# First halves of x and W0 turned by TensorE, every 4th channel in a k tile, and product 5 by output tile, in a two-layer LoRA kernel on one core

## The chip, the cores and the metric

The kernel runs on one core of one Trainium2 chip. The metric is the device time of one execution in microseconds (us); lower is better. The time of a kernel is the median over its runs.

## The reference

Two layers are applied one after the other to x, 8 rows of 256 tokens with 1024 channels, all in float32:

```
x = x + L0(x): base = x @ W.T                    # W: 1024 x 1024
      logits = x @ Wr.T + 5 * one_hot(language)  # 8 experts
      gates  = softmax over the two largest logits, 0 for the other experts
      lora   = ((x @ A[e].T) * gates[e]) @ B[e].T summed over e   # rank 16
      L0     = base + 2 * lora
x = x + x @ weight[adapter_id].T                 # one of 16 matrices, 1024 x 1024, for each of the 8 rows
```

## The kernel before, in words

**Precision.** Every operand of a large product is split into a high part (ScalarE copies it to the rounded matmul type, `high`, L965) and a low part (VectorE subtracts the high part, `low`, L583). A product step is three matmuls of 128x128 by 128x512: high by high, high by low, low by high (L1227 to L1229). Where a term is its own input added on (`x +`), ones are added to the diagonal of the weight matrix (`add_diagonal`, L572; for the second layer `add_ones` on GpSimd, L501).

**Layer 0.** The 2048 tokens are worked in two spans of 1024. Within a span the 1024 x 1024 by 1024 x 1024 product is cut into halves in each direction and done by a Strassen scheme with seven products, in the order 1, 2, 6, 7, 5, 4, 3. Each product has four output tiles r and four k tiles k, so 16 steps of 3 matmuls. Of span 0, products 1, 2 and 6 run r outside and k inside ("by tile", the rest run k outside and need all four weight pieces of the product at their first step). s1 to s4 and t1 to t4 are the sums and differences of the quarters of W0 and x that the scheme wants. `features` (L1220) computes x @ A.T and the logits with full float32 matmuls; `make_gates` makes the gates on VectorE; `turn_gated` (L1259) turns the gated features on TensorE, `gT_high` and `gT_low` split them (L987, L692), and `lora` (L1238 to L1241) adds the low-rank part to a quarter. `add_up` (L715) adds a finished quarter's parts, `copy_u3` (L1007) copies a bank out.

**Channels on the partitions.** Both operands need the channel of the contraction on the partitions. Rows of x, W0, A, Wr and of the second layer's matrices are loaded in four bands of 256 channels, each to its 32 partitions (`fill`, `fill_x`, L421 and L428), and VectorE turns 32x32 blocks (STREAM_TRANSPOSE, L545 for halves, L566 for whole tiles, L559 and L759 for A and Wr, L730 for the second layer). k tile m holds the channels q*256 + m*32 + j, and a block's 32 channels lie side by side.

**Start.** TensorE runs 30 matmuls on the identity (`WARM`, L1206). The first halves of the four x tiles and of W0's tile 0 are loaded by the queues of SyncE and ScalarE, turned by VectorE (`turn_half`, L545), split, and product 1 starts. While product 1 runs, W0's tiles 1 to 3 come one by one: VectorE turns a tile, adds the diagonal, and it is split.

**Layer 1.** 64 tiles of the chosen matrices are loaded by SyncE's queue, get their diagonal on GpSimd, are turned (L730) and split (L1066 on ScalarE, L736 on VectorE). VectorE gives one tile the pair L730 and L736. The result of layer 0 comes back from HBM and is split too (L1057, L720). For each row and each half of the outputs there are two output tiles of 24 matmuls (L1349 to L1351), which need the four tiles of their group. ScalarE copies results out (L1083) and stores them.

All engines run lists written out by hand, in order; the order of VectorE's and ScalarE's lists is the schedule.

Of the kernel before, what the change touches and what calls it, by code (L numbers as in the profile page):

```python
# [5 lines left out]
def cond_resid_kernel(nc, x, lang_ids, adapter_ids, w0, wr, a, b, w1, out):  # L6
# [7 lines left out]
    NB, T, D = x.shape  # L14
    E, R, _ = a.shape
    NA = w1.shape[0]
    P = 128
# [14 lines left out]
    WARM = 30  # L32
# [15 lines left out]
    def by_tile(s, i):  # L48
        return s == 0 and i in (1, 2, 6)
# [9 lines left out]
    def x_item(s, h, t):  # L59
# [14 lines left out]
    FRONT = ([("xh", t, 0) for t in range(XT)] + [("wh", 0, 0)] + [("w", r) for r in range(1, HM)] + [("a",)] +  # L74
             [("xh", t, 1) for t in range(XT)] + [("wh", 0, 1)])
# [6 lines left out]
    SLOT["wh", 0, 0] = SLOT["wh", 0, 1] = W0_PLACES[0]  # L82
# [17 lines left out]
    for i in (5, 4, 3):  # L100
        PIECES += [("bd",)] if i == 4 else []
        PIECES += [("u", i, r) for r in range(HM)] + [("x", 0, i, k) for k in range(HM)]
# [24 lines left out]
    with ctx:  # L127
# [104 lines left out]
        def sides(p):  # L232

            kind = p[0]
            if kind in ("xl", "xr"):
                t, h = p[1], kind == "xr"
                cut, ms = slice(t * P, (t + 1) * P), slice(h * HM, (h + 1) * HM)
                return (half_x(0, t, h).rearrange("p (m f) -> p m f", m=HM), early_hi[:, ms, cut], early_lo[:, ms, cut])
            if kind in ("wl", "wr"):
                i, r = (1, p[1]) if kind == "wl" else (2, p[1])  # L240
                return turned_wf[:, r, (i - 1) * HALF:i * HALF], u_whole(i, 0)[:, r], u_whole(i, 1)[:, r]
# [33 lines left out]

        def b_ps():
            return banks[:, 4:6, :]
# [17 lines left out]
        x_loaded = [[sem(f"x{'lr'[h]}{pair}_loaded") for h in range(2)] for pair in range(2)]  # L295
        w_half_loaded = [sem(f"w0{'lr'[h]}_loaded") for h in range(2)]
# [119 lines left out]
        def x_raw(t):  # L416
            return turned_wf[:, HM + t]

        def fill(engine, slot, rows, signal, parts=range(Q), j=slice(0, DQ)):
            for c in parts:  # L420
                engine.dma_start(raw_tile(slot)[c * S:(c + 1) * S, :].rearrange("p (q j) -> p q j", q=Q)[:, :, j],  # L421
                                 rows[:, :, c * DQ:(c + 1) * DQ][:, :, j]).then_inc(signal, 16)

        def fill_x(engine, pair, h, parts=range(Q)):
            rows = x_rows[pair * 2 * P:(pair + 1) * 2 * P, :].rearrange("(n s) d -> s n d", s=S)
            for c in parts:
                dst = turned_wf[c * S:(c + 1) * S, HM + 2 * pair:HM + 2 * pair + 2, :]
                engine.dma_start(dst.rearrange("p t (q j) -> p (t q) j", q=Q)[:, :, h * P:(h + 1) * P],  # L428
                                 rows[:, :, c * DQ + h * P:c * DQ + (h + 1) * P]).then_inc(x_loaded[pair][h], 16)

        def fill_w_half(engine, h, parts=range(Q)):
            fill(engine, W0_PLACES[0], w0_rows(0), w_half_loaded[h], parts, slice(h * P, (h + 1) * P))

        def w0_rows(m):
            return w0.rearrange("(q m s) d -> m s q d", m=M, s=S)[m]
# [4 lines left out]
        def _(sp):  # L440
# [27 lines left out]
            fill_x(sp, 0, 0, (0, 1))  # L468
            fill_x(sp, 1, 0, (0, 1))
            fill_w_half(sp, 0, (0, 1))  # L470
# [3 lines left out]
            fill_x(sp, 0, 1)  # L474
            fill_x(sp, 1, 1)
            fill_w_half(sp, 1)
# [8 lines left out]
        def _(pool):  # L485
# [28 lines left out]
            def make_s3(r):  # L514
                pool.wait_ge(transposed, TURN_AT["w", HM + r] + 1)
                pool.wait_ge(lo_done, PIECE_AT["wl", r] + 1)
                if r == 0:
                    pool.wait_ge(t2_done, XT)
# [16 lines left out]
        def _(dve):  # L535
            def turn_half(item):
                kind, n, h = item
                if kind == "xh":
                    dve.wait_ge(x_loaded[n // 2][h], Q * 16)
                    src, dst = x_raw(n), tokens_f[:, n]  # L540
                else:
                    dve.wait_ge(w_half_loaded[h], Q * 16)
                    src, dst = raw_tile(SLOT[item]), turned_wf[:, n]
                ms = slice(h * HM, (h + 1) * HM)
                nc.vector.transpose(dst.rearrange("p (m q s) -> p q m s", m=M, q=Q)[:, :, ms],  # L545
                                    src.rearrange("p (q m j) -> p q m j", q=Q, m=M)[:, :, ms]).then_inc(transposed, 1)

            def turn(item):
# [9 lines left out]
                if item[0] == "a":  # L558
                    nc.vector.transpose(fac[:, :, 0:ER].rearrange("p m (q s) -> p q m s", q=Q),  # L559
                                        src.rearrange("p (q m j) -> p q m j", q=Q, m=M)).then_inc(transposed, 1)  # L560
# [5 lines left out]
                nc.vector.transpose(dst.rearrange("p (m q s) -> p q m s", m=M, q=Q),  # L566
                                    src.rearrange("p (q m j) -> p q m j", q=Q, m=M)).then_inc(transposed, 1)

            def add_diagonal(m):
                dve.wait_ge(transposed, TURN_AT[("w", m) if m else ("wh", 0, 0)] + 1)  # L570
                ones = turned_wf[:, m, m * P:(m + 1) * P]
# [151 lines left out]
            def turn_w1(n):  # L723
# [15 lines left out]
            turn_half(("xh", 0, 0))  # L739
            turn_half(("xh", 1, 0))  # L740
            low(("xl", 0))
            low(("xl", 1))
            turn_half(("xh", 2, 0))
            turn_half(("xh", 3, 0))
            low(("xl", 2))
            turn_half(("wh", 0, 0))
# [632 lines left out]
```

## Time and profile before

| | |
|---|---|
| median of 3 runs | 404.14 us (402.94 to 404.2) |
| the profiled execution | 401.46 us, its span 399.7 us |
| TensorE busy | 391.1 us, 98% |
| VectorE busy | 310.2 us, 78% |
| ScalarE busy | 173.8 us, 43% |
| GpSimd busy | 52.9 us, 13% |
| granted TensorE clock | 1.0 |

The span is what the trace covers, from 0 to 399.7 us; the execution's own time is 1.8 us longer. A busy share is the time in which an instruction of the engine was in work. Matmuls overlap, so each is listed with a longer duration than the step from one to the next.

### The profile page before, as it was taken

The numbers are of one execution on the slowest core, as the hardware profiler recorded it, in microseconds if no ns is written. First come the engines' busy times: TensorE is split into PE (matmuls) and PEld (weight loads), VectorE is DVE, ScalarE is ACT, GpSimd is POOL, SyncE is SP. The second block draws the span as 40 slices with busy tenths as digits, with TensorE's granted clock in tenths as the row PEclk, the third lists the DMA queues.
The fourth block names the chain that finished last, engine by engine and source line by source line (L and its number), as shares of the span: only waits on it lengthen the run. The fifth ranks groups of instructions, "written<-read, shape, count | busy, mean of one in ns | idle before, by whom it ended". The sixth has DMA issues, their size and how long they took to land.

```text
span 399.7 us, 5958 instructions
## 1 busy us (share of the span) xinstructions
PE 391.1 (98%) x1900; PEld 330.0 (83%) x1900; DVE 310.2 (78%) x419; ACT 173.8 (43%) x245; POOL 52.9 (13%) x81
## 2 busy tenths in 40 slices
PE   8899999799999999999999999999999999999996
PEld 8698988588889888888888888878888888888886
DVE  5899998997457568229877956999999999999900
ACT  3352263754220143335355333655555555656511
POOL 1005300000000100000110211442232120323000
PEclk9999999999999999999999999999999999999999
DMA  9998750033476400006492999999999999999232
GB/s 208 227 200 209 106 161 2 0 107 106 137 202 204 91 1 0 2 0 197 136 289 117 229 261 247 281 250 267 271 274 282 266 277 282 272 260 235 66 93 52
DMA packets 87553, 68.60 MB, mean 172 GB/s; under 512 B 16322, under 2 KB 86498, under 8 KB 87010
## 3 DMA queue, kind: packets, MB, share of 16 engines
q1 hardware_dynamic: 60832, 46.55, 49.8%
q10 hardware_dynamic: 26690, 21.67, 18.3%
q8 instruction: 15, 0.25, 0.3%
q14 instruction: 16, 0.13, 0.1%
HBM read 53.51 MB, written 14.68 MB: 171 GB/s over the span
## 4 chain that ended last, share of the span: by engine, by line
PE 94%; DVE 2%; ACT 1%; DMA 1%; issue 0%; ACTq 0%; DVEq 0%
PE banks L1349 15%; PE banks L1350 15%; PE banks L1351 15%; PE banks L1227 13%; PE banks L1228 12%; PE banks L1229 12%; PE banks L1220 7%; PE banks L1238 2%; PE banks L1240 2%; PE banks L1241 2%; DMA turned_w_f<-in_x_dram 1%; DVE weights L583 1%; ACT weights L965 0%; DVE turned_w_f L628 0%; PE banks L1259 0%; DVE tokens_f L545 0%
## 5 line engine op out<-in xcount | busy, mean ns | idle before, releaser
L1227 PE MATMUL banks<-ring,weights 128*128 128x512 f32 x192 | 75.2, 392 | 2.4 <-DVE stage L715 2.4
L1349 PE MATMUL banks<-weights,tokens 128*128 128x512 f32 (+1 forms) x184 | 70.0, 380 | 0.0
L1351 PE MATMUL banks<-weights,tokens 128*128 128x512 f32 (+1 forms) x184 | 69.9, 380 | 0.0
L1350 PE MATMUL banks<-weights,tokens 128*128 128x512 f32 (+1 forms) x184 | 69.9, 380 | 0.0
L1066 ACT ACTIVATE weights<-weights_f 128x1024 fp32r<-128x1024 f32 x44 | 46.5, 1060 | 52.7 <-DVE weights_f L730 49.8
L730 DVE STREAM_TRANSPOSE weights_f<-raw 128x1024 f32<-128x1024 f32 x42 | 51.8, 1235 | 6.1 <-POOL raw L501 5.6
L501 POOL TENSOR_TENSOR raw<-raw,ident 128x128 f32<-128x128 f32 x42 | 26.0, 619 | 216.0 <-DMA raw<-in_L_cond_weight_dram 216.0
L736 DVE TENSOR_TENSOR weights<-weights_f,weights 128x1024 fp32r<-128x1024 f32 x44 | 52.3, 1190 | 0.9 <-ACT weights L1066 0.9
L1229 PE MATMUL banks<-ring,turned_w 128*128 128x512 f32 x128 | 49.8, 389 | 0.0
L1228 PE MATMUL banks<-tokens,weights 128*128 128x512 f32 x128 | 49.8, 389 | 0.0
L1227 PEld LDWEIGHTS banks<-ring,weights 128*128 128x128 f32 x192 | 36.0, 188 | 10.1 <-DVE tokens L583 2.8
L1349 PEld LDWEIGHTS banks<-weights,tokens 128*128 128x128 f32 x184 | 34.6, 188 | 7.0 <-issue 0.4
L1351 PEld LDWEIGHTS banks<-weights,tokens 128*128 128x128 f32 x184 | 34.6, 188 | 6.6
L1350 PEld LDWEIGHTS banks<-weights,tokens 128*128 128x128 f32 x184 | 34.6, 188 | 6.5
L965 ACT ACTIVATE ring<-tokens_f 128x512 fp32r<-128x512 f32 x40 | 22.5, 621 | 29.2 <-PE banks L1229 25.1
L1066 ACT ACTIVATE turned_w<-weights_f 128x1024 fp32r<-128x1024 f32 x20 | 21.2, 1060 | 23.6 <-DVE weights_f L730 23.5
L1349 PE MATMUL banks<-turned_w,tokens 128*128 128x512 f32 x80 | 31.1, 389 | 0.0
L1350 PE MATMUL banks<-turned_w,tokens 128*128 128x512 f32 x80 | 31.1, 389 | 0.0
L1351 PE MATMUL banks<-turned_w,tokens 128*128 128x512 f32 x80 | 31.1, 389 | 0.0
L730 DVE STREAM_TRANSPOSE weights_f<-ring_f 128x1024 f32<-128x1024 f32 x22 | 27.1, 1233 | 5.1 <-POOL ring_f L501 5.1
L1220 PEld LDWEIGHTS banks<-fac,tokens_f 128*128 128x128 f32 x256 | 30.0, 190 | 0.3
L1220 PE MATMUL banks<-fac,tokens_f 128*128 128x136 f32 x256 | 30.1, 279 | 0.0
(127 smaller groups left out, 613.8 us busy)
## 6 DMA issues: line engine op xcount, KB each, us to landing
raw<-in_L_cond_weight_dram SPq DMA_DIRECT2D x168, 128.0 KB, 5.2
ring_f<-in_L_cond_weight_dram SPq DMA_DIRECT2D x88, 128.0 KB, 5.8
out_dram<-sums ACTq DMA_DIRECT2D x31, 256.0 KB, 7.0
raw<-in_x_dram SPq DMA_DIRECT2D x48, 128.0 KB, 3.7
x_kept<-stage ACTq DMA_DIRECT2D x24, 256.0 KB, 3.2
raw<-in_L_cond_W_dram SPq DMA_DIRECT2D x16, 128.0 KB, 3.2
turned_w_f<-in_x_dram SPq DMA_DIRECT2D x12, 128.0 KB, 6.6
ring_f<-in_L_cond_W_dram SPq DMA_DIRECT2D x12, 128.0 KB, 5.4
```

Source lines behind the costliest of these rows:

```text
L501: nc.gpsimd.tensor_tensor(spot, spot, ident[:].rearrange("p (q j) -> p q j", q=Q), ALU.add)\
L730: nc.vector.transpose(w1_turn(n).rearrange("p (m q s) -> p q m s", m=M, q=Q), raw_tile(SLOT[item]).rearrange("p (q m j) -> p q m j", q=Q, ...
L736: nc.vector.tensor_tensor(w1_dest(n, 1), w1_turn(n).rearrange("p (m f) -> p m f", m=M), w1_dest(n, 0).bitcast(F32), ALU.subtract).then_inc ...
L965: nc.scalar.activation(sides(p)[1], sides(p)[0], ACT.Copy).then_inc(hi_done, 1)
L1066: nc.scalar.activation(w1_dest(n, 0), w1_turn(n).rearrange("p (m f) -> p m f", m=M), ACT.Copy)\
L1220: mm = nc.tensor.matmul(ps, xT[:, m, :], fac[:, m, 0:FC], start=m == 0, stop=m == M - 1)
L1227: nc.tensor.matmul(ps, u_hi, x_hi, start=first and k == 0, stop=False, skip_group_check=True)
L1228: nc.tensor.matmul(ps, u_hi, x_lo, start=False, stop=False, skip_group_check=True)
L1229: nc.tensor.matmul(ps, u_lo, x_hi, start=False, stop=k == HM - 1, skip_group_check=True)\
L1349: nc.tensor.matmul(ps, x_hi, w_hi, start=m == 0, stop=False)
L1350: nc.tensor.matmul(ps, x_hi, w_lo, start=False, stop=False)
L1351: mm = nc.tensor.matmul(ps, x_lo, w_hi, start=False, stop=m == M - 1)
```

## The change

**Start.** The first halves of x's four tiles are loaded as they lie, 128 tokens on the partitions, one DMA of 256 KB for a tile, two on each queue. W0's left half of output tile 0 comes the same way in four DMAs. TensorE turns them by 4 transposes of 128x128 for each (`turn_left`), x into the banks 4 to 7, W0's into bank 3; `high`, `low` and `add_diagonal(0)` read these banks. ScalarE later copies the five banks to where the turned halves used to be (`copy_left`). The 30 identity matmuls become 6, 2 and 6, around the transposes. Five of VectorE's half-tile transposes go.

**Channels.** k tile (h, m) holds the channels q*256 + h*128 + 4*j + m. The loads of full tiles keep their form, but each block that VectorE turns (x, W0, A, Wr, and all 64 tiles of layer 1) is now read with a step of four words (16 bytes) between neighbouring elements; what it writes is unchanged in form. W0's rows for an output tile are every 4th row. The copy that puts B in order (L1120) becomes 8 copies of 128 columns in place of 4 of 256.

**Product 5 of span 0** runs by output tile. VectorE's and ScalarE's lists are put in another order around it: the x pieces of product 5 are split before or between the u pieces, `add_up` of quarter "11" and `copy_u3` are spread between the u pieces, and the sum for the "12" quarter of B (`sum_bd`, its high and low part) is moved behind the pieces of product 4. ScalarE does three `copy_u2` before the x pieces of product 7, in place of two.

```
-    WARM = 30
+    WARM = (6, 2, 6)
-        return s == 0 and i in (1, 2, 6)
+        return s == 0 and i in (1, 2, 6, 5)
...
+        def fill_x_left(engine, t):
+            engine.dma_start(x_left(t).rearrange("p (c j) -> p c j", c=Q),
+                             x_rows[t * P:(t + 1) * P, :].rearrange("p (c j) -> p c j", c=Q)[:, :, 0:P])\
+                .then_inc(xl_loaded[t], 16)
+        def fill_w_left(engine, parts):
+            for q in parts:
+                engine.dma_start(w_left()[q * S:(q + 1) * S, :].rearrange("p (c j) -> p c j", c=Q),
+                                 w0[q * DQ:q * DQ + P:HM, :].rearrange("p (c j) -> p c j", c=Q)[:, :, 0:P])\
+                    .then_inc(wl_loaded, 16)
...
-            return w0.rearrange("(q m s) d -> m s q d", m=M, s=S)[m]
+            return w0.rearrange("(q h s m) d -> h m s q d", h=2, m=HM, s=S)[m // HM, m % HM]
...
+            def by_block(src):
+                return src.rearrange("p (q h j m) -> p q h m j", q=Q, h=2, m=HM)
...
-                nc.vector.transpose(dst.rearrange("p (m q s) -> p q m s", m=M, q=Q),
-                                    src.rearrange("p (q m j) -> p q m j", q=Q, m=M)).then_inc(transposed, 1)
+                nc.vector.transpose(dst.rearrange("p (h m q s) -> p q h m s", h=2, m=HM, q=Q), by_block(src))\
+                    .then_inc(transposed, 1)
...
-                nc.vector.transpose(w1_turn(n).rearrange("p (m q s) -> p q m s", m=M, q=Q),
-                                    raw_tile(SLOT[item]).rearrange("p (q m j) -> p q m j", q=Q, m=M))\
+                nc.vector.transpose(w1_turn(n).rearrange("p (h m q s) -> p q h m s", h=2, m=HM, q=Q),
+                                    by_block(raw_tile(SLOT[item])))\
...
             make_gates(0)
             low(("b",))
             make_s1(0)
+            low(("x", 0, 5, 0))
             gT_low(0)
+            low(("u", 5, 0))
+            low(("x", 0, 5, 1))
+            add_up(0, "11", 0)
+            low(("x", 0, 5, 2))
+            low(("x", 0, 5, 3))
             make_s1(1)
             make_s1(2)
-            low(("u", 5, 0))
+            low(("u", 5, 1))
+            add_up(0, "11", 1)
             make_s1(3)
-            for r in range(1, HM):
-                low(("u", 5, r))
+            low(("u", 5, 2))
+            add_up(0, "11", 2)
+            low(("u", 5, 3))
+            add_up(0, "11", 3)
...
+            def copy_left(n):
+                p = ("xl", n) if n < XT else ("wl", 0)
+                act.wait_ge(lo_done, PIECE_AT[p] + 1)
+                nc.scalar.activation(half_x(0, n, 0) if n < XT else quarter_w(7, 0), left_bank(n), ACT.Copy)\
+                    .then_inc(xl_copied if n < XT else wl_copied, 1)
...
+            def turn_left(src, n):
+                for m in range(HM):
+                    turn_m = nc.tensor.transpose(left_bank(n)[:, m * P:(m + 1) * P],
+                                                 src[:, m::HM], ident[:])
+                turn_m.then_inc(left_turned, 1)
...
+            def product_5():
+                for r in range(HM):
+                    pe.wait_ge(lo_done, PIECE_AT["u", 5, r] + 1)
+                    pe.wait_ge(summed_up, added_at(0, "11", r) + 1)
+                    for k in range(HM):
+                        if r == 0 and k:
+                            pe.wait_ge(lo_done, PIECE_AT["x", 0, 5, k] + 1)
+                        step(0, 5, k, r, side_bank(0, r), True)
```

## Rows read from the trace of the kernel before

**Rows 1.** The page: busy time of the engines; VectorE's busy tenths in 40 slices.

```profile
PE 391.1 (98%) x1900; PEld 330.0 (83%) x1900; DVE 310.2 (78%) x419; ACT 173.8 (43%) x245; POOL 52.9 (13%) x81
...
DVE  5899998997457568229877956999999999999900
```

**Rows 2.** The chain that ended last, in order of time: start, length, what.

```profile
1.22 3.50 DMA turned_w_f<-in_x_dram
...
10.18 0.30 DVE turned_w_f L572
10.51 0.64 ACT weights L965
11.17 0.70 DVE weights L583
11.92 0.50 PE banks L1227
...
12.66 0.23 PE banks L1229
...
396.52 0.38 ACT sums L1083
```

**Rows 3.** Who waited for whom, whole span: us in total, times, longest.

```profile
PE banks L1227 <- DVE stage L715: 2.4, 1, 2.4
...
PEld banks L1227 <- DVE weights L583: 2.3, 4, 1.5
```

**Rows 4.** Timeline of the start: start, duration, engine, line; "q" is an issuing queue.

```profile
2.71 0.95 ACTq L421 DMA_DIRECT2D ring_f<-in_L_cond_W_dram  x2
...
8.69 1.57 ACTq L1094 DMA_DIRECT2D sums<-in_L_cond_Wr_dram  x4
```

**Rows 5.** DMA issues from 0 to 40 us: KB each, median us from issue to landing.

```profile
ring_f<-in_L_cond_W_dram ACTq DMA_DIRECT2D x2, 64.0 KB, 4.7
```

**Rows 6.** Timeline of TensorE's 8 transposes of B (eight instructions merged).

```profile
54.59 1.03 PE L1249 MATMUL banks<-ident,raw 128*128 128x128 f32 x8
```

**Rows 7.** TensorE in stretches of 1 us: busy (instructions), granted clock, DMA share, GB/s.

```profile
4.70:5.70 1.00, 1.00 (x7) 1.00 1.16 275
...
7.70:8.70 1.00, 1.00 (x11) 1.00 1.12 232
```

**Rows 8.** Timeline around the start of product 5 of span 0.

```profile
70.16 1.03 ACT L987 ACTIVATE lora_g<-banks 128x1024 fp32r<-128x1024 f32 x1 [5.22 <-PE banks L1259]
...
71.22 1.22 DVE L692 TENSOR_TENSOR lora_g<-banks,lora_g 128x1024 fp32r<-128x1024 f32 x1 [0.70 <-ACT lora_g L987]
...
75.22 0.39 PE L1241 MATMUL banks<-lora_g,lora_b 128*128 128x512 f32 x1
...
76.57 0.69 DVE L583 TENSOR_TENSOR tokens<-tokens_f,ring 128x512 fp32r<-128x512 f32 x1
77.17 2.48 DVE L715 TENSOR_TENSOR stage<-banks,sums 128x512 f32<-128x512 f32 x4
...
78.00 0.47 PE L1227 MATMUL banks<-ring,weights 128*128 128x512 f32 x1 [2.40 <-DVE stage L715]
```

**Rows 9.** VectorE's groups by form: count, busy us, mean ns, idle before.

```profile
L736 DVE TENSOR_TENSOR weights<-weights_f,weights 128x1024 fp32r<-128x1024 f32 x44 | 52.3, 1190 | 0.9 <-ACT weights L1066 0.9
L730 DVE STREAM_TRANSPOSE weights_f<-raw 128x1024 f32<-128x1024 f32 x42 | 51.8, 1235 | 6.1 <-POOL raw L501 5.6
...
L545 DVE STREAM_TRANSPOSE tokens_f<-turned_w_f 128x512 f32<-128x512 f32 x8 | 5.2, 688 | 4.7 <-DMA turned_w_f<-in_x_dram 4.7
```

**Rows 10.** ScalarE's groups by form: the copy of B, and the copy of half a result.

```profile
L1120 ACT ACTIVATE weights_f<-banks 128x256 f32<-128x256 f32 x4 | 1.2, 391 | 1.3 <-PE banks L1249 1.3
L1083 ACT ACTIVATE sums<-banks 128x256 f32<-128x256 f32 x2 | 0.8, 384 | 4.7 <-PE banks L1351 4.7
```

**Rows 11.** GpSimd's groups by form: its subtractions of x's halves.

```profile
L511 POOL TENSOR_TENSOR tokens_f<-tokens_f 128x512 f32<-128x512 f32 x4 | 5.2, 1296 | 17.8 <-DVE weights L583 13.5 <-DVE weights_f L605 4.4
```

**Rows 12.** Timeline of VectorE at its end.

```profile
376.33 2.42 DVE L736 TENSOR_TENSOR weights<-weights_f,weights 128x1024 fp32r<-128x1024 f32 x2
```

More of the change, by code:

```diff
@@ L294, in cond_resid_kernel @@
         raw_loaded = [sem(f"raw_loaded{s}") for s in range(RAW1)]
-        x_loaded = [[sem(f"x{'lr'[h]}{pair}_loaded") for h in range(2)] for pair in range(2)]
-        w_half_loaded = [sem(f"w0{'lr'[h]}_loaded") for h in range(2)]
+        xl_loaded = [sem(f"xl{t}_loaded") for t in range(XT)]
+        xr_loaded = [sem(f"xr{pair}_loaded") for pair in range(2)]
+        wl_loaded = sem("wl_loaded")
+        wr0_loaded = sem("wr0_loaded")
+        left_turned = sem("left_turned")
+        xl_copied = sem("xl_copied")
+        wl_copied = sem("wl_copied")
         w_loaded = [sem(f"w{r}_loaded") for r in range(HM)]
@@ L431, in fill_w_half, with x_left, x_right, w_left @@
-        def fill_w_half(engine, h, parts=range(Q)):
-            fill(engine, W0_PLACES[0], w0_rows(0), w_half_loaded[h], parts, slice(h * P, (h + 1) * P))
+        def x_left(t):
+            return turned_wf[:, HM + 2 * (t // 2), t % 2 * HALF:(t % 2 + 1) * HALF]
+        def x_right(t):
+            return turned_wf[:, HM + 2 * (t // 2) + 1, t % 2 * HALF:(t % 2 + 1) * HALF]
+        def w_left():
+            return raw_tile(W0_PLACES[0])[:, 0:HALF]
+        def w_right():
+            return raw_tile(W0_PLACES[0])[:, HALF:D]
@@ new lines, in fill @@
+        def fill(engine, slot, rows, signal):
+            for c in range(Q):
+                engine.dma_start(raw_tile(slot)[c * S:(c + 1) * S, :].rearrange("p (q j) -> p q j", q=Q),
+                                 rows[:, :, c * DQ:(c + 1) * DQ]).then_inc(signal, 16)
+        def fill_x_left(engine, t):
+            engine.dma_start(x_left(t).rearrange("p (c j) -> p c j", c=Q),
+                             x_rows[t * P:(t + 1) * P, :].rearrange("p (c j) -> p c j", c=Q)[:, :, 0:P])\
+                .then_inc(xl_loaded[t], 16)
@@ new lines, in fill_x_right @@
+        def fill_x_right(engine, pair):
+            rows = x_rows[pair * 2 * P:(pair + 1) * 2 * P, :].rearrange("(n s) d -> s n d", s=S)
+            for c in range(Q):
+                engine.dma_start(turned_wf[c * S:(c + 1) * S, HM + 2 * pair + 1, :].rearrange("p (n j) -> p n j", j=P),
+                                 rows[:, :, c * DQ + P:(c + 1) * DQ]).then_inc(xr_loaded[pair], 16)
+        def fill_w_left(engine, parts):
[3 more added lines that the diff above has]
+                    .then_inc(wl_loaded, 16)
@@ L840, in span @@
                 else:
-                    sum_bd()
                     for t in range(XT):
                         make_t4(0, t)
-                    low(("bd",))
                     lows("u", 4)
@@ L851, in span @@
                     turn_w1(5)
+                else:
+                    sum_bd()
+                    low(("bd",))
                 for r in range(HM):
@@ L1096, in _ @@
             act.dma_start(lang_i[:], lang_ids.partition_broadcast(P)).then_inc(lang_loaded, 16)
-            for r in range(1, HM):
+            for r, lefts in ((1, (XT, 0)), (2, (1, 2)), (3, (3,))):
                 high(("wl", r))
                 high(("wr", r))
+                for n in lefts:
+                    copy_left(n)
             copy_p1(0, 0)
@@ L1204, in _, with warm @@
             pe.wait_ge(consts, 3)
-            for _ in range(WARM):
-                nc.tensor.matmul(banks[:, 0, 0:P], ident[:], ident[:], start=True, stop=True)
+            def warm(count):
+                for _ in range(count):
+                    nc.tensor.matmul(banks[:, 0, 0:P], ident[:], ident[:], start=True, stop=True)
+            def turn_left(src, n):
[3 more added lines that the diff above has]
+                turn_m.then_inc(left_turned, 1)
+            warm(WARM[0])
+            for t in range(XT):
+                pe.wait_ge(xl_loaded[t], 16)
+                turn_left(x_left(t), t)
+                if t == 1:
+                    warm(WARM[1])
+            pe.wait_ge(wl_loaded, Q * 16)
+            turn_left(w_left(), XT)
+            warm(WARM[2])
             def features(s, h):
```

174 lines of the change are left out of this document (93 added, 81 removed).

## The prediction

> **What bounds the kernel now.** I read the page first: TensorE is busy 98% of the span [rows 1]. So a gain can only come from the places where its product work waits. The chain in order of time gives the first: product 1 starts at 11.92 us [rows 2], and what TensorE does before that are identity matmuls without use. The waits give the others: 2.4 us before product 5 of span 0, for `add_up`, and 2.3 us in 4 waits for low parts of W0, of which 1.5 is the one before product 1, so 0.8 us lies in three gaps inside it [rows 3]. Behind 78 us no wait of TensorE on another engine shows. The fourth thing to see is VectorE's line of slices: it stands at 9 from 20 to 60 us and from 250 to 380 us [rows 1]. It is the second bound, and nearly all its transposes lie in these stretches. All that the change can give is 11.92 - 4.72 us of landing and splitting, 0.8 and 2.4; what it can take is in VectorE's slices.
>
> **The change part by part.** The sum is made against the profiled execution, 401.46 us; the median of the runs is 404.14, 2.7 us (0.7%) above it, and I carry the difference over to it.
>
> *Start.* Now the first x pair lands at 1.22 + 3.50 = 4.72 us [rows 2]; its bytes are the same in the new form (two DMAs of 256 KB in place of four of 128 KB), so I keep 4.7. VectorE then did 5 half transposes of 0.69 us [rows 9], 3.4 us, and they go. The chain doesn't shrink by all of it, since the last to come is W0's left half: issued at 2.71 to 3.66 us [rows 4], landed 4.7 us later [rows 5], so at 7.5 to 8.3; I take 8.0. Four transposes follow: the 8 of B take 1.03 us, about 0.11 us from one to the next and 0.27 for the last [rows 6], so 0.6 us here, 8.6. `add_diagonal` 0.30 [rows 2], 8.9 to 9.0. ScalarE's `high` of W0 stands behind the issue of four DMAs for Wr, 1.57 us [rows 4], and these can go out only when the `high` of the last x half is given out, about 7.8 (the 512 KB of x tiles 2 and 3 come at 275 GB/s [rows 7], so 1.9 us after the first two, at 6.6, and their transposes and the `high` of tile 2 stand before it). That gives 9.4. Then 0.64 and 0.70 us [rows 2]: 10.75, and product 1 at 10.8 in place of 11.92. Gain 1.1 us. Bounds: 2.0 if W0 is there at 7.5 and the queue isn't in the way; nothing, or a loss of 0.5, if the x tiles come a microsecond later.
>
> Inside product 1 the cadence stays: VectorE's chain of turn, diagonal, two lows sets it, so the three gaps of 0.27 us stay too. ScalarE gets 5 `copy_left` of 0.6 us [nearest: 0.38 for half the columns, rows 10] in a stretch in which it had over 1.5 us idle in each round of 2.9; hidden. If they weren't, each would push the next `high` by what is over.
>
> *The clock at the start.* With 30 identity matmuls TensorE did 7 instructions in 1 us until 5.7 us and 11 at 7.7 us, while the granted clock reads 1.00 in both, the 2.4 GHz level [rows 7]. So its first 4 us of work were slow in fact. The new kernel leaves TensorE idle between its 6, 2 and 6 matmuls, and product 1 may meet the slow pace. By the ratio 7 to 11, 2 us of its matmuls at the slow pace are 0.7 us late, of which the gaps take part. I take nothing for it in the sum and keep 0 to 2.7 us (all 12 matmuls of the first output tile at twice 0.23 us [rows 2]) for the range.
>
> *Product 5.* The lora matmuls end at 75.22 + 0.23 = 75.45; product 5 starts at 78.00, one start-up late. VectorE was the cause: `gT_low` till 72.4, then 3 `make_s1`, 4 lows of u, the low of x at 76.57 and the first `add_up` at 77.17 to 77.8 [rows 8]. In the new list VectorE does, behind `gT_low` (72.4), low u0, low x1 and `add_up` 0, each 0.61 us apart (4 `add_up` in 2.48 us [rows 8]): 74.2. `add_up` 0 needs the third lora matmul, at 73.6, so it doesn't wait. x2 and x3 are ready at 75.4. TensorE wants k = 2 at 75.45 + 6 x 0.23 = 76.8. `add_up` 1 stands behind two sums and one low: 77.9, wanted at 75.45 + 12 x 0.23 = 78.2. `add_up` 2 79.7, wanted 80.9; `add_up` 3 80.9, wanted 83.7. So product 5 starts at once, and the thinnest margin is 0.3 us at the second output tile. Gain 78.00 - 75.45 = 2.5 us. Next in line is product 4 at 75.45 + 11 + 2.8 = 89.2: `make_t4` to 83.3, the four lows of u4 to 86.4, x4 by 88.9, of which the first is wanted at 89.2. `sum_bd` behind them costs 0.6 us and a high and low before the `add_up` of "22", due only before product 3. Hidden. Bounds: 1.5 (the margin of 0.3 and that of product 4 both missed by half a microsecond) to 2.6.
>
> *B.* Eight copies of 128 columns in place of four of 256: the fixed part of a copy comes four times more, some 0.6 us on ScalarE, before an x piece that waited 1.3 us for TensorE anyway. Nothing.
>
> *W0 rows every 4th, DMA issues.* Same bytes and pieces, same number on the queues. Nothing.
>
> *Reads with a step of 16 bytes.* 64 transposes of layer 1 at 1235 ns [rows 9], and all those of layer 0, read single words. No transpose in the trace does. The nearest row is the copy of B: it reads its bank with 512 bytes between neighbours and takes 391 ns for 256 columns, against 384 for the same number read side by side [rows 10]: 7 ns, 2%. It is another engine and PSUM. Below: nothing; side by side, 512 more elements take 1235 - 688 = 547 ns [rows 9], and no mechanism makes a stepped read faster than that. Above: the slowest wide row of the trace, 1296 ns for 512 elements on GpSimd [rows 11], 2.5 ns an element, so 2.6 us for a transpose, 1.4 more than now. I take nothing, the row it is nearest to, and the rest is a rival.
>
> Sum: 1.1 + 2.5 = 3.6 us, 401.46 - 3.6 = 397.9 for a profiled execution, 404.14 - 3.6 = **400.5 us** for the median, 0.9% faster.
>
> **Rivals.**
>
> *The stepped read is slow (slower).* Mechanism: VectorE fetches one word where it fetched its neighbours with it, and every element of a transpose costs more. VectorE ends at 376.33 + 2.42 = 378.8 [rows 12]; TensorE's last group of 48 matmuls starts at 396.5 - 48 x 0.23 = 385.5 [rows 2]. That is a slack of 6.7 us, and L730 has 6.1 us of waits for GpSimd before it [rows 9], 12.8 in all, over some 56 transposes of layer 1: from 12.8 / 56 = 0.23 us more per transpose on VectorE decides. If each element took a second slot, 547 x 2 = 1.1 us more, layer 1 would be late by 56 x 1.1 - 12.8 = 49 us; some 15 transposes before 60 us, where VectorE's slices read 9, add 14 or so. 404.1 - 3.6 + 63 = 464 us. At a third of that price it is 404.1 - 3.6 + 8 + 5 = 414, at the upper bound of 1.4 us 404.1 - 3.6 + 66 + 18 = 485. For it: VectorE has no reserve in both stretches. Against: the copy of B. Chance 0.2.
>
> The Trainium skill speaks for this rival. "Vector Engine (DVE) Microarchitecture Reference", section 5 with the SBUF access granule, says that a port keeps its full rate only for runs of at least two neighbouring words, and gives 1.73 ns a column against 1.05 for one source that hops at every element; it also has a one-source case that hopped and kept the full rate. By 1.73 a transpose would be an estimated 0.7 us longer and the kernel some 435 us. The row of the copy of B doesn't agree with it, but is of PSUM; no row here shows VectorE doing it in SBUF.
>
> *The gains are given back (no change).* TensorE meets product 1 at the slow pace (up to 2.7 us) and the first x tiles come no earlier, or product 5's second tile waits: 3.6 falls to 1 or less, 403.2 to 404.5. For: 7 against 11 instructions. Against: the last 6 identity matmuls and the transposes lie right before product 1. Chance 0.14.
>
> *A small loss.* The copies out of the banks stand before a `high` of W0's tiles in ScalarE's list and stretch product 1's rounds, and the start gives nothing: 405 to 407. Chance 0.04.
>
> *The change does what it says:* 0.62.
>
> **How the numbers follow.** Forecast 400.5, own range 398.3 to 402.7: 5.2 us (both upper bounds, 2.0 and 2.6, and part of the 0.8) down to a gain of 1.5 (start eaten by the clock). What a measurement of this kernel can tell from no change is 0.3%, 1.2 us. Faster 0.62, within it 0.14, slower 0.24. The range 398.0 to 405.5 leaves out the stepped read, 0.2.
>
> **What would show it.** Right: product 1 at about 10.8 us; L730's mean at 1.24 us; no wait of TensorE at L715 near 75 us, and no new one before product 5's second tile and product 4. Wrong: L730 at 1.4 us or more, VectorE at 9 up to the end and TensorE's matmuls of layer 1 waiting for it; fewer than 11 instructions of TensorE a microsecond around 10 us and first matmuls of product 1 0.4 us apart.

## The result and the profile after

The changed kernel takes 438.06 us (median; 437.61 to 439.84) against 403.6 us for the kernel before: 1.087 times as long, 95% interval 1.083 to 1.090. The prediction was 400.5 us, faster. It was wrong, and the stepped read, which it had put down as a rival with 2 in 10, is what happened.

The page of the changed kernel: busy time of the engines, the slices of VectorE and of the granted clock, and the share of the chain that ended last.

```profile
PE 402.4 (92%) x1888; PEld 334.6 (77%) x1888; DVE 370.9 (85%) x414; ACT 175.9 (40%) x254; POOL 52.4 (12%) x81
...
DVE  3999999897776864198899899999999999999940
...
PEclk9999999999999999999999999899998999989899
...
PE 47%; DVE 29%; issue 15%; DMA 5%; SPq 2%; ACT 1%; POOL 0%; ACTq 0%; DVEq 0%; POOLq 0%
```

TensorE fell from 98% to 92% busy [rows 1]; VectorE has 61 us more of work with 5 instructions fewer, and it now makes up 29% of the chain. The clock's slices show something new: in layer 1 the granted clock falls below full speed in places.

VectorE's groups by form in the changed kernel (count, busy us, mean ns, idle before); L770 and L578 are the rows to set beside L730 and L545 [rows 9].

```profile
L770 DVE STREAM_TRANSPOSE weights_f<-raw 128x1024 f32<-128x1024 f32 x42 | 84.7, 2018 | 2.4 <-POOL raw L534 1.8
L776 DVE TENSOR_TENSOR weights<-weights_f,weights 128x1024 fp32r<-128x1024 f32 x44 | 53.2, 1209 | 0.0
L770 DVE STREAM_TRANSPOSE weights_f<-ring_f 128x1024 f32<-128x1024 f32 x22 | 44.5, 2022 | 0.0
...
L602 DVE STREAM_TRANSPOSE tokens_f<-raw 128x1024 f32<-128x1024 f32 x12 | 23.8, 2004 | 5.2 <-PE banks L1311 3.0 <-DMA raw<-in_x_dram 2.2
...
L578 DVE STREAM_TRANSPOSE tokens_f<-turned_w_f 128x512 f32<-128x512 f32 x4 | 4.2, 1080 | 0.0
```

A whole transpose went from 1235 to 2018 ns, a half one from 688 to 1080: 0.77 ns more for each element, wherever the tile lies. The subtraction L776, whose reads are as before, stays at 1.2 us. So it isn't VectorE that is slower, it is this read.

What TensorE waited for in the changed kernel (us in total, times, longest):

```profile
PE banks L1445 <- issue: 18.0, 6, 3.3
PE banks L1309 <- DVE weights L623: 6.0, 7, 1.7
PE banks L1309 <- DVE tokens L623: 2.8, 2, 1.6
...
PE banks L1302 <- issue: 1.0, 1, 1.0
```

The 2.4 us before product 5 [rows 3] are gone; nothing waits for L755, the new line of `add_up`. In its place stand 6.0 us in seven waits for low parts of W0 and its sums (0.7 us of them before product 1), 2.8 us in two waits for low parts of x, and 18.0 us in six waits before matmuls of layer 1. The view names no releaser for these six, but each ends 0.1 us behind a low part made by VectorE in L776, as here:

```profile
381.21 1.24 DVE L776 TENSOR_TENSOR weights<-weights_f,weights 128x1024 fp32r<-128x1024 f32 x1
...
382.55 0.77 PE L1445 MATMUL banks<-weights,tokens 128*128 128x512 f32 x1 [3.23 <-issue]
```

Behind five of the six waits the granted clock falls to the 1.2 GHz level for a few microseconds, with TensorE's matmuls 0.43 us apart in place of 0.23. Behind the wait just shown, TensorE alone (busy, instructions, granted clock, DMA share, GB/s):

```profile
382.00:384.00 2.00, 1.45 (x4) 0.55 0.94 268
384.00:386.00 2.00, 2.00 (x7) 0.59 0.54 138
```

By these readings one fall costs 1.7 us (0.45 and 0.41 of the full speed missing in two stretches of 2 us), and the five cost 8.5. Two longer stretches of the changed kernel, in the same columns:

```profile
234.00:266.00 32.00, 32.00 (x143) 1.00 1.10 266
...
300.00:350.00 50.00, 44.11 (x179) 0.93 0.91 230
```

and VectorE at its end:

```profile
417.14 2.43 DVE L776 TENSOR_TENSOR weights<-weights_f,weights 128x1024 fp32r<-128x1024 f32 x2
```

VectorE ends at 419.6 us, in place of 378.8 [rows 12]: 40.8 us later, while the span is 36.8 us longer. The slack was eaten first.

The start of the changed kernel, by its chain in order of time, and product 5 by its timeline:

```profile
9.75 0.60 ACT weights L1013
...
10.38 0.69 DVE weights L623
11.07 1.92 DVE turned_w_f L602
```

```profile
84.10 0.39 PE L1323 MATMUL banks<-lora_g,lora_b 128*128 128x512 f32 x1
...
84.33 0.39 PE L1309 MATMUL banks<-ring,weights 128*128 128x512 f32 x1
```

W0's left half is split by 11.07, 0.8 us earlier than before (11.87 by [rows 2]); from there the chain runs through L602, the stepped transposes of W0's other tiles. Product 5 starts 0.23 us behind the last lora matmul, at full pace. The time was lost elsewhere, by VectorE's transposes.

### The profile page after: what moved, and what is told of

It is laid out like the page before. It is cut to its first block, busy times and chain, and to the rows that moved or that the text cites. A ratio compares the mean times of both kernels' runs of the same rounds, so it can differ in the third digit from the quotient of the medians.

```text
span 436.5 us, 5942 instructions
## 1 busy us (share of the span) xinstructions
PE 402.4 (92%) x1888; PEld 334.6 (77%) x1888; DVE 370.9 (85%) x414; ACT 175.9 (40%) x254; POOL 52.4 (12%) x81
## 4 chain that ended last, share of the span: by engine, by line
PE 47%; DVE 29%; issue 15%; DMA 5%; SPq 2%; ACT 1%; POOL 0%; ACTq 0%; DVEq 0%; POOLq 0%
PE banks L1309 8%; PE banks L1310 8%; PE banks L1311 8%; DVE weights_f L770 6%; DVE weights L776 6%; DMA raw<-in_L_cond_weight_dram 5%; PE banks L1445 5%; PE banks L1446 4%; PE banks L1447 4%; PE banks L1302 3%; DVE turned_w L776 3%; DVE turned_w_f L602 3%; DVE weights L623 2%; SPq L442 2%; DVE tokens_f L602 2%
## 5 line engine op out<-in xcount | busy, mean ns | idle before, releaser
L770 DVE STREAM_TRANSPOSE weights_f<-raw 128x1024 f32<-128x1024 f32 x42 | 84.7, 2018 | 2.4 <-POOL raw L534 1.8
L1445 PE MATMUL banks<-weights,tokens 128*128 128x512 f32 (+1 forms) x184 | 72.3, 393 | 11.8 <-issue 11.8
L1120 ACT ACTIVATE weights<-weights_f 128x1024 fp32r<-128x1024 f32 x44 | 46.5, 1059 | 74.6 <-DVE weights_f L770 74.6
L1446 PE MATMUL banks<-weights,tokens 128*128 128x512 f32 (+1 forms) x184 | 71.8, 390 | 0.0
L1447 PE MATMUL banks<-weights,tokens 128*128 128x512 f32 (+1 forms) x184 | 71.7, 390 | 0.0
L534 POOL TENSOR_TENSOR raw<-raw,ident 128x128 f32<-128x128 f32 x42 | 24.6, 587 | 241.1 <-DMA raw<-in_L_cond_weight_dram 241.1
L776 DVE TENSOR_TENSOR weights<-weights_f,weights 128x1024 fp32r<-128x1024 f32 x44 | 53.2, 1209 | 0.0
L1445 PEld LDWEIGHTS banks<-weights,tokens 128*128 128x128 f32 x184 | 35.7, 194 | 20.2 <-issue 13.4
L770 DVE STREAM_TRANSPOSE weights_f<-ring_f 128x1024 f32<-128x1024 f32 x22 | 44.5, 2022 | 0.0
L1447 PEld LDWEIGHTS banks<-weights,tokens 128*128 128x128 f32 x184 | 35.8, 194 | 7.0
L1446 PEld LDWEIGHTS banks<-weights,tokens 128*128 128x128 f32 x184 | 35.8, 195 | 6.9
L1445 PE MATMUL banks<-turned_w,tokens 128*128 128x512 f32 x80 | 32.7, 409 | 7.1 <-issue 6.2
L1120 ACT ACTIVATE turned_w<-weights_f 128x1024 fp32r<-128x1024 f32 x20 | 21.2, 1059 | 37.7 <-DVE weights_f L770 37.7
L1446 PE MATMUL banks<-turned_w,tokens 128*128 128x512 f32 x80 | 32.6, 408 | 0.0
L1447 PE MATMUL banks<-turned_w,tokens 128*128 128x512 f32 x80 | 32.4, 404 | 0.0
```

Source lines behind the costliest of these rows:

```text
L534: nc.gpsimd.tensor_tensor(spot, spot, ident[:].rearrange("p (q j) -> p q j", q=Q), ALU.add)\
L770: nc.vector.transpose(w1_turn(n).rearrange("p (h m q s) -> p q h m s", h=2, m=HM, q=Q), by_block(raw_tile(SLOT[item])))\
L776: nc.vector.tensor_tensor(w1_dest(n, 1), w1_turn(n).rearrange("p (m f) -> p m f", m=M), w1_dest(n, 0).bitcast(F32), ALU.subtract).then_inc ...
L1120: nc.scalar.activation(w1_dest(n, 0), w1_turn(n).rearrange("p (m f) -> p m f", m=M), ACT.Copy)\
L1445: nc.tensor.matmul(ps, x_hi, w_hi, start=m == 0, stop=False)
L1446: nc.tensor.matmul(ps, x_hi, w_lo, start=False, stop=False)
```

## The experiments

Ratios are against the kernel before on the same chip, whose median was 402.7 to 403.5 us, with 95% intervals. Seven of the kernels read channels in an order that doesn't fit the rest, as their expectations say; the work of all engines stays the same in number and size. The kernel of experiment 3 is called kernel 3 below.

**1. Only layer 1 reads side by side again** (the changed kernel, one edit).

```
-   transpose(w1_turn(n) as "p (h m q s) -> p q h m s", by_block(raw_tile))
+   transpose(w1_turn(n) as "p (m q s) -> p q m s", raw_tile as "p (q m j) -> p q m j")
```

> The changed kernel with one edit: the 64 transposes of layer 1 read side by side again. The second layer's contraction then pairs other channels, so that the result is another one; all instructions, sizes and waits are the same. Theory (the stepped read costs VectorE time): L770 falls from 2.02 to 1.24 us; layer 1 costs what it did before, so only the part lost up to 125 us stays (6.4 us by the start of features of span 1): 409 to 411 us. Rival (the loss in layer 1 comes from the memory side, W0's rows or the DMAs, and the step of the read costs nothing): stays at 436 to 440.

Measured 407.92 us, ratio 1.015 (1.012 to 1.018), a little under the 409 to 411 expected. L770 takes 1.23 us, L602 still 2.00. 438.06 - 407.92 = 30.1 us of the loss hang on the read of 64 transposes. No wait of TensorE in layer 1 is left and the clock reads 1.00. In the changed kernel, the waits that layer 1's transposes caused are 18.0, 0.9 and 1.6 us, and the falls of the clock 8.5: 29.0 of the 30.1.

**2. Only layer 1 stepped** (the kernel before, the reverse edit).

> The kernel before with one edit: the 64 transposes of layer 1 read with a step of 16 bytes (the result is then another one). Theory: the transpose takes 2.02 in place of 1.24 us, 56 x 0.78 - 12.8 = 31 us later, so 434 us, and TensorE's granted clock falls below 1.0 in layer 1. Rival: 403.6 as before.

Measured 432.36 us, ratio 1.076 (1.072 to 1.079), 29.7 us more than the kernel before. TensorE's waits of layer 1 are there without any other part of the change, and so is the lower clock, 0.976 in the mean:

```profile
PE banks L1349 <- issue: 15.7, 6, 3.7
PE banks L1227 <- DVE stage L715: 2.4, 1, 2.4
```

**3. All of VectorE's reads side by side** (the changed kernel with `by_block`, `turn_right`, the read of Wr and layer 1 side by side).

> The changed kernel with all of VectorE's transposes reading side by side (x, W0, A, Wr and layer 1; the channels no longer fit together, so the result is another one). The rest of the change stays: start by TensorE, product 5 by tile. Theory: all of the loss goes and the forecast of the prediction comes true, 403.6 - 3.6 = 400.0 us (398.5 to 401.5). Rival (the start by TensorE or the longer ScalarE list loses too): above 403.

Measured 398.19 us, ratio 0.990 (0.988 to 0.992), a little better than the range expected. Nothing of the loss is left; the other parts gain 1.0%, against the 0.9% forecast (experiment 4 shows that a part of it is the clock's). The stepped read in layer 0 cost 407.92 - 398.19 = 9.7 us, of which TensorE's new waits in layer 0 (those of the changed kernel) are 7.5: 5.3 for W0 and its sums inside and behind product 1, 1.2 for x and 1.0 before `features`.

**4. Product 5 alone** (the kernel before with product 5 by tile and the two lists in the new order).

```
-        return s == 0 and i in (1, 2, 6)
+        return s == 0 and i in (1, 2, 6, 5)
...
+            low(("x", 0, 5, 0))
             gT_low(0)
+            low(("u", 5, 0))
+            low(("x", 0, 5, 1))
+            add_up(0, "11", 0)
```

> The kernel before with product 5 of span 0 by output tile and the lists of VectorE and ScalarE around it in the new order, nothing else. Theory: the wait of 2.4 us before product 5 goes and nothing takes its place: 403.6 - 2.5 = 401.1 us. Rival (it is given back at the second output tile or at product 4): no difference, 403 to 404.

> The kernel of product_5_only once more, beside step_of_8_bytes on one chip: 399.5 to 401 us.

Measured 399.53 us, ratio 0.993 (0.990 to 0.995), where 401.1 was expected, and in the second run 399.34 us, 0.992 (0.989 to 0.995). No wait of TensorE stands at the second output tile or at product 4. In the second run's timeline the start of product 5 stands where the prediction had put it, at 75.45:

```profile
75.23 0.39 PE L1257 MATMUL banks<-lora_g,lora_b 128*128 128x512 f32 x1
75.45 0.39 PE L1243 MATMUL banks<-ring,weights 128*128 128x512 f32 x1
```

The gain is more than the wait of 2.4 us that went. Of the 18 executions of the kernel before beside the second run, 14 have a mean granted clock of 0.992 to 0.996 and a median of 403.8 us; 4 have 1.000 and 401.4 us, and the profiled execution of the kernel before is of this kind. All six of product 5 alone have 0.998 or more, with 399.3 us: 2.1 us less than the 401.4. Where the clock is lost shows in the trace of experiment 5, whose kernel still has the wait before product 5 (mean clock 0.996), in its timeline and in two stretches of TensorE alone:

```profile
77.31 0.47 PE L1293 MATMUL banks<-ring,weights 128*128 128x512 f32 x1 [2.40 <-DVE stage L754]
```

```profile
78.00:80.00 2.00, 2.00 (x7) 0.54 0.00 0
80.00:82.00 2.00, 2.00 (x7) 0.61 1.01 336
```

Behind the wait the clock falls to the 1.2 GHz level, which by these readings costs 1.7 us. The trace of experiment 2 has the same fall (0.69 and 0.50 in these two stretches). The trace of the kernel before has the same wait and no fall, so it doesn't follow in every execution. The new order takes away the wait and, with it, this fall. Others remain: the kernel of experiment 8 runs product 5 the same way and has 0.994 to 0.996 in 4 of its 12 executions; where wasn't looked into.

**5. The start by TensorE alone, side by side** (kernel 3 with product 5 put back).

> The kernel of all_side_by_side with product 5 and its lists put back as before: what stays is the start by TensorE with all of VectorE's reads side by side (channels don't fit together, another result). Theory: product 1 starts 0.5 to 0.8 us earlier and the start is worth that or a little more, 402.7 - 0.8 = 401.9 us (401.2 to 402.5). Rival (the start is worth what the prediction said, 1.1 us, and more with the gaps inside product 1): 401.0.

Measured 401.99 us against 403.0, ratio 0.998 (0.996 to 1.000): 0.8 us, near the edge of what can be told from nothing. Between the executions with a clock of 0.998 or more it is 0.3 us (401.3 against 401.6). In its profiled execution product 1 started at 11.25 us, 0.7 earlier. In six profiled executions of kernels with the old start (the kernel before, and experiments 2, 4 and 6) it started at 11.9 us four times and at 12.8 twice, the latter where the first x pair landed at 8.2 us in place of 4.7; so single executions scatter as much as the gain.

**6. How much VectorE can lose in layer 1.** The kernel before with the stepped read in every 4th and in every 2nd tile:

```
+                if n % 4 == 0:        # n % 2 == 0 in the other
+                    transpose(..., raw_tile as "p (q h j m) -> p q h m j")
```

> The kernel before; of layer 1's 64 transposes every 4th (n % 4 == 0) reads with a step of 4 words (another result). The slack of VectorE in layer 1 was read as 12.8 us, and 14 x 0.77 = 10.8 us of extra work lie under it. Theory (slack, then one to one): no difference, 402.7 (within 1.2 us). Rival (every extra microsecond of VectorE there shows, since the pace of the pair of turn and low sets TensorE's groups): 402.7 + 10.8 = 413.

> The same with every 2nd tile (n % 2 == 0): 28 x 0.77 = 21.6 us of extra work. Theory (slack of 12.8 us, then one to one): 402.7 + 9 = 411.5 us (409 to 413). Rival (no slack): 424.

Measured 403.66 us, ratio 1.003 (1.000 to 1.005), and 414.03 us, ratio 1.026 (1.021 to 1.032), a little over the 409 to 413 expected; its four executions lie between 411.4 and 417.3. With experiment 2 that is a curve, with the extra work of VectorE estimated as 14, 28 and 56 transposes of 0.77 us: 10.8 us cost about 1, which can hardly be told from nothing, 21.6 cost about 11, 43 cost 30. TensorE's new waits in layer 1 agree: 1.4 us in all, 10.0 us, and in experiment 2 over 17. So some 11 to 14 us are free or nearly so, and the rest goes about one to one.

**7. The price of a step, by itself.** A kernel with single instructions on 128 x 1024 float32. Each stands on its own line:

```
L96 to L101: transpose, read with a step of 1, 2, 4, 8, 16, 32 words     L102: written with a step of 4
L103, L104, L105: 256 columns: pairs 8 words apart, single words 4 apart, side by side
L106, L107: transpose out of PSUM, step 4 and step 1
L109 to L112: subtraction plain, one source, both sources, the result with step 4; L113: PSUM source with step 4
L125 to L127: ScalarE copy plain, read with step 4, written with step 4; L128, L129: out of PSUM, step 1 and 4
L82, L83: GpSimd copy plain, read with step 4
L139, L141: TensorE transposes, stationary operand with step 1 and 4
```

> A kernel of its own: only single instructions on 128 x 1024 float32, one line each, 6 times. VectorE transposes that read with a step of 1, 2, 4, 8, 16 and 32 words, one that writes with a step of 4, 256 columns in pairs of neighbours 8 words apart against 256 single words 4 apart, and a PSUM source at steps 1 and 4; VectorE subtractions with one source, both, the result or a PSUM source stepped by 4; copies on ScalarE and GpSimd at steps 1 and 4; TensorE transposes with a stationary operand at steps 1 and 4. Theory (a word that is not read with its neighbour costs VectorE extra, about 0.77 ns each): steps of 2 words and more take 2.0 us against 1.24, pairs take as long as side by side, and PSUM and ScalarE show no or little difference. Rival (the price grows with the distance, by lines of 16 bytes): step 2 takes 1.24 to 1.5 us, 4 takes 2.0, and 8 to 32 more.

Its groups by form (count, busy us, mean ns, idle before):

```profile
L126 ACT ACTIVATE ac<-src 128x1024 f32<-128x1024 f32 x6 | 12.1, 2022 | 0.2
L99 DVE STREAM_TRANSPOSE dv<-src 128x1024 f32<-128x1024 f32 x6 | 12.0, 2006 | 0.2
L98 DVE STREAM_TRANSPOSE dv<-src 128x1024 f32<-128x1024 f32 x6 | 11.9, 1987 | 0.2
L102 DVE STREAM_TRANSPOSE dv<-src 128x1024 f32<-128x1024 f32 x6 | 11.9, 1979 | 0.2
...
L83 POOL COPY po<-src 128x1024 f32<-128x1024 f32 x6 | 11.9, 1975 | 0.4
L110 DVE TENSOR_TENSOR dv<-src,oth 128x1024 f32<-128x1024 f32 x6 | 11.8, 1972 | 0.2
L111 DVE TENSOR_TENSOR dv<-src,oth 128x1024 f32<-128x1024 f32 x6 | 11.8, 1970 | 0.2
L101 DVE STREAM_TRANSPOSE dv<-src 128x1024 f32<-128x1024 f32 x6 | 11.4, 1903 | 0.2
L100 DVE STREAM_TRANSPOSE dv<-src 128x1024 f32<-128x1024 f32 x6 | 11.4, 1892 | 0.2
L106 DVE STREAM_TRANSPOSE dv<-ps 128x1024 f32<-128x1024 f32 x6 | 7.5, 1250 | 0.2
L107 DVE STREAM_TRANSPOSE dv<-ps 128x1024 f32<-128x1024 f32 x6 | 7.5, 1250 | 0.2
L96 DVE STREAM_TRANSPOSE dv<-src 128x1024 f32<-128x1024 f32 x6 | 7.5, 1245 | 0.2
L97 DVE STREAM_TRANSPOSE dv<-src 128x1024 f32<-128x1024 f32 x6 | 7.5, 1245 | 0.2
...
L104 DVE STREAM_TRANSPOSE dv<-src 128x256 f32<-128x256 f32 x6 | 3.8, 627 | 0.2
...
L103 DVE STREAM_TRANSPOSE dv<-src 128x256 f32<-128x256 f32 x6 | 2.7, 446 | 0.2
```

Read it by lines. Step 1 and step 2 (8 bytes) take the same 1245 ns, and steps of 4 to 32 words all take 1.9 to 2.0 us. So neither the theory (step 2 pays as well) nor the rival (the price grows with the distance) was right: there is one jump between 8 and 16 bytes. Pairs cost nothing (446 ns, as the 445 side by side). Writing with a step costs the same as reading with one. ScalarE and GpSimd pay it too, with 2022 and 1975 ns against 1058 and 1041 side by side. And out of PSUM a step of 4 words costs nothing: 1250 ns at both steps on VectorE, and 1026 and 1025 on ScalarE. GpSimd wasn't tried there. TensorE's stationary operand doesn't pay in any way that counts (its weight loads read 206 and 211 ns). A step of 3 words wasn't tried.

**8. The whole change with a step of 8 bytes.** If 8 bytes are free, the change can have its layout and VectorE its pace.

```
-                return src.rearrange("p (q h j m) -> p q h m j", q=Q, h=2, m=HM)
+                return src.rearrange("p (q h g j i) -> p q h g i j", q=Q, h=2, g=2, i=2)
...
-            engine.dma_start(x_left(t)...,                      # 4 pieces of 512 bytes a row
+            for g in range(2):
+                engine.dma_start(x_left(t)...[:, g],            # 4 pieces of 256 bytes a row
...
-                                                 src[:, m::HM], ident[:])
+                                                 src[:, m // 2 * 2 * P + m % 2:(m // 2 + 1) * 2 * P:2], ident[:])
```

> The whole change with another order of the channels: k tile (h, g, i) holds the channels q*256 + h*128 + g*64 + 2*j + i, so that VectorE's transposes and TensorE's stationary operands read with a step of 2 words (8 bytes). The price: the left halves come in pieces of 256 bytes in place of 512, in twice as many DMAs, and the copy of B is 16 copies of 64 columns. It computes the reference. Theory (8 bytes are free, as in step_prices): L602 and L770 take 1.24 us, and the whole gain is there, 403 - 4 = 399 us, less what the smaller pieces cost at the start (up to 1 us): 398.3 to 400. Rival (the finer DMA pieces or B's copies eat more than the start gives): 400 to 402.

Measured 400.51 us, ratio 0.994 (0.992 to 0.996): 37.6 us better than the change as made, and the transposes are back at their price (L772 is the one of layer 1):

```profile
L772 DVE STREAM_TRANSPOSE weights_f<-raw 128x1024 f32<-128x1024 f32 x42 | 51.7, 1234 | 7.0 <-POOL raw L536 6.5
```

But it isn't faster than product 5 alone. Its chain in order of time shows why:

```profile
5.40 5.41 DMA ring_f<-in_L_cond_W_dram
10.85 0.76 PE banks L1282 x4
12.04 0.61 ACT weights L1015
12.67 0.70 DVE weights L625
```

W0's left half now lands at 10.8 us, so product 1 starts at 13.4, later than before the change (11.9). The rival of that expectation holds, as to the start. The row shows which part of it: the last DMA of W0's left half goes out at 5.40 us and lands 5.41 us later, where in experiment 5 it goes out at 3.07 and lands 5.57 later. The 2.3 us lie before it goes out, behind the issue of twice as many DMAs, and not between its issue and its landing.

**9. The identity matmuls** (kernel 3 with 6, 0 and 0 of them in place of 6, 2 and 6).

> The kernel of all_side_by_side with 6, 0 and 0 identity matmuls in place of 6, 2 and 6. Theory (the slow pace of TensorE's first 4 us is a matter of how long it has been at work, so less work before product 1 leaves product 1 at the slow pace for a while): the first matmuls of product 1 stand 0.4 us apart and the time is 1 to 2.5 us above 398.2. Rival (TensorE's pace has nothing to do with these matmuls): 398.2.

Measured 399.38 us, ratio 0.991 (0.988 to 0.994), against 0.990 (0.988 to 0.992) with all of them. By the time it can't be told. The five executions have a mean clock from 0.999 (397.9 us) down to 0.990 (400.6 us). The profiled one is the slowest and does show the slow pace (TensorE alone is the first figure; the granted clock stands behind GpSimd's):

```profile
6.00:8.00 2.00, 0.27 (x3) 0.25 (x3) 1.29 (x2) 0.66 (x2) 0.00 (x0) 1.00 1.20 240
...
10.00:12.00 2.00, 0.86 (x4) 0.46 (x3) 0.89 (x2) 1.00 (x2) 0.00 (x0) 0.50 1.12 223
...
14.00:16.00 2.00, 2.00 (x7) 1.57 (x6) 1.27 (x4) 1.59 (x4) 0.00 (x0) 0.55 1.14 228
```

TensorE was idle most of 6 to 8 us, the clock read 0.50 (the 1.2 GHz level) from 10 to 14 us, and the first matmuls of product 1 stood 0.43 us apart. In the same execution an x tile landed at 8.8 us, which delays the start by itself, and TensorE was idle again for 2.1 us right before product 1. The identity matmuls aren't needed for an explanation. The first profiled execution of product 5 alone (experiment 4) has all 30 of them and shows the same. Its first x pair landed at 8.2 us, TensorE was idle for 2.1 us before product 1 at 12.8, the clock read 0.50 from 13 to 16 us, and the first matmuls stood 0.43 us apart. What the two have in common is late data and an idle TensorE; whether leaving out identity matmuls makes it more frequent isn't shown.

## Why the prediction was wrong, and where it was right

**The step that failed** is the one under "Reads with a step of 16 bytes": "I take nothing, the row it is nearest to". The row was the copy of B by ScalarE [rows 10], 391 against 384 ns at a step of 512 bytes. It is true, and it is a row of PSUM, where experiment 7 shows neither VectorE nor ScalarE paying for a step of 16 bytes. The read that changed is one of SBUF, where a step of 16 bytes costs VectorE, ScalarE and GpSimd 0.7 to 1.0 ns an element. The text had named both differences, another engine and PSUM. The engine didn't matter, the memory did. Of the bounds kept, nothing and 1.4 us more a transpose, the truth was 0.78, in the middle; with ends so far apart and VectorE without reserve, the choice of the end carried the whole forecast, and 2 in 10 was too little for a mechanism that nothing in the trace excluded. The signs that it had named for being wrong all came: L770 over 1.4 us, VectorE's slices mostly at 9 up to the end, and TensorE's matmuls of layer 1 waiting for it.

The rule of the Trainium skill cited there ("Vector Engine (DVE) Microarchitecture Reference", the SBUF access granule) spoke the right way: an estimated 0.7 us more by it, 0.78 measured, and some 435 us against 438. Experiment 7 agrees with it on pairs and on the size, and differs in one point: a step of two words has no neighbours side by side either, and is free.

**The rival's working held.** With its own formula and the measured 0.78 us: 56 x 0.78 - 12.8 = 31 us for layer 1 (30.1 and 29.7 measured in experiments 1 and 2), 15 x 0.78 = 12 for layer 0, at most (9.7). 404.1 - 3.6 + 31 + 10 = 441 against 438. Only its size, 1.1 us a transpose, was 40% too high. The point from which VectorE decides, 0.23 us a tile or 12.8 us in all, lies in experiment 6 between 10.8 us (about 1 lost) and 21.6 (11 lost). That it fits is in part luck. The 6.1 us of waits for GpSimd are those of one form of L730; its other form has 5.1 more:

```profile
L730 DVE STREAM_TRANSPOSE weights_f<-ring_f 128x1024 f32<-128x1024 f32 x22 | 27.1, 1233 | 5.1 <-POOL ring_f L501 5.1
```

With both, the slack would have come to 17.9 us. The runs show 11 to 14, so a part of this idle time could not be used; which part wasn't looked into.

**Product 5.** Right in mechanism and time: 2.5 us forecast, 75.45 as the start, found so; no new wait at the second tile or at product 4. The kernel gains 3.0 to 3.2 us (0.7% to 0.8%) by the ratios. 2.1 us of it are there at the same granted clock; the rest is the fall of the clock behind the old wait (experiment 4), which the prediction didn't have.

**The start.** Forecast 1.1 us, measured 0.8 (experiment 5; 0.3 at the same clock), with product 1 at 11.1 to 11.4 us in place of 10.8. The term that was too small is the landing of the last x tile (6.6 forecast): it was the chain's release at 1.47 + 6.12 = 7.59 us in kernel 3,

```profile
1.47 6.12 DMA turned_w_f<-in_x_dram
7.59 0.04 issue
7.63 0.76 PE banks L1274 x4
```

and from there the `high` of x, the four DMAs of Wr and the `high` of W0 follow as described. W0's left half was late too, at 8.65 us in place of 8.0, and in experiment 5 its landing is what the chain goes through. The three gaps in product 1 stayed, as forecast: in kernel 3 the weight loads wait 0.24, 0.28 and 0.25 us before W0's tiles 1 to 3, with 2.87 us from one to the next as before.

**B's copies, W0's rows, `copy_left`, the clock.** Taken at nothing, and kernel 3, which has all of them, shows no cost of theirs. Its granted clock was 0.998 to 1.000, and against executions of the kernel before at such a clock it takes 398.2 us for 401.5, 3.3 us less where 3.6 were forecast. Product 5 and the start by themselves add up to less, 2.1 and 0.3 us at such a clock; the other 0.9 us isn't explained, and single executions scatter by as much. The feared slow pace at the start is real, but it comes in some executions of the old start as well (experiments 4 and 9), so it isn't a price of the change alone.

**The 2.7 us carried over.** The prediction took the difference between the profiled execution and the median, 401.46 and 404.14, as a constant. It is mostly the clock: in the kernel before, executions at 0.992 to 0.996 take 403.8 us and those at 1.000 take 401.4. Kernel 3 has none of the former, so its gain by the medians, 4.5 us, is more than its parts give at the same clock.

**The rest of the sum.** -4.5 us (kernel 3) + 9.7 (layer 0 stepped) + 30.1 (layer 1 stepped) = 35.3, against 34.5 measured. This sum is no test, since each term is a difference of neighbouring kernels; what it is off by is the difference between two medians of the kernel before, 402.7 and 403.6. The test is experiment 2, which puts layer 1's part on the kernel before by itself and finds 29.7. In layer 1 a part of the loss is TensorE's own, through the clock: 8.5 of the 30.1 us by its readings.

**The range.** Its lower end, 398.3 us, doesn't follow from the 5.2 us given for it: 404.14 - 5.2 = 398.9. Nothing hangs on it here.

**The version that beats both** is product 5 alone: 399.3 to 399.5 us, 0.992 to 0.993 of the kernel before. Kernel 3's 398.2 us can't be had as it is, since its channels don't fit together. `turn_left` turns rows as they lie, with evenly spaced columns; with 512-byte pieces these are 4 apart, and in the one version with 2 apart the pieces are 256 bytes (experiment 8). Whether another layout has both wasn't tried.

## What to carry to other kernels

When a change touches how every instance of an instruction reads its operand, price that read before anything else, and count the instances on the engine with the least reserve: 3.6 us of good scheduling stood against 83 transposes of whole tiles. A row that is to stand in for an unseen one has to share the memory, not only the shape; if it doesn't, measure the read alone, which takes one small kernel. If a layout needs a step between float32 words in SBUF, look for one of 8 bytes, or do the reordering on a read from PSUM. And before a median is compared with a single profiled execution, look at the granted clock of both: a wait on TensorE can cost more than its own length.

## What the runs showed of the hardware that was not expected

- A step costs by whether it is over 8 bytes, not by how far it goes: transposes of 128 x 1024 take 1245 ns at 1 and 2 words, 1987 at 4, 2006 at 8, 1892 at 16, 1903 at 32.
- It costs once: one stepped source, two, or a stepped result of a subtraction all take 1.97 to 1.98 us in place of 1.23.
- PSUM is exempt for VectorE and ScalarE, at 16 bytes (1250 and 1250 ns, 1025 and 1026 ns).
- A wait of TensorE can cost more than its length: behind the 2.4 us before product 5 the granted clock read 0.54 and 0.61 in the next two stretches of 2 us, 1.7 us more (experiment 5); in the changed kernel five such falls cost 8.5 us. It doesn't follow each wait.
- The clock column reads 1.00 in the first microseconds, while TensorE does 7 identity matmuls from 4.7 to 5.7 us and 11 from 7.7 to 8.7 us [rows 7]; in experiment 9 it reads 0.50 after an idle stretch, and there the matmuls of product 1 stand 0.43 us apart in place of 0.23.
